# Expert coefficients spread by broadcast loads, the score shift as a bias column, and the order listed anew

## What is computed

```python
x = x + 0.5 * ffn(layernorm(x))
x = x + attn(layernorm(x))        # 16 heads of 8, rotary q and k, ALiBi, full softmax, proj
x = x + 0.5 * ffn(layernorm(x))

def ffn(xf):
    scores = sigmoid(xf @ gate.T)               # 8 experts in 2 groups; the better group is kept
    sel, top = top 2 of (scores + corr_bias) inside the kept group, top normalised to sum 1
    lat = xf @ fc1_w.T                           # 64
    routed = sum over sel of top * (relu(lat @ w1[e].T)**2 @ w2[e].T) @ fc2_w.T
    shared = relu(xf @ up_w.T)**2 @ down_w.T     # 512 wide
    return routed + shared
```

## Time and profile before

| | us |
|---|---|
| median of 3 runs (807.15 to 807.88) | 807.54 |
| profiled execution, its own time | 807.31 |
| span of the profile | 805.5 |
| head, until the first exp starts | 83.85 |
| first to last exp start (256 exps) | 660.8 |
| last exp's start (744.62) to the end of the span | 60.9 |

### The profile page before, as it was taken

One profiled execution on the slowest core, in us unless ns is written; L12 is line 12 of the kernel. 1 busy time (PEld: TensorE's weight loads), 2 busy tenths in 40 slices (PEclk: granted clock), 3 DMA queues, 4 the chain that ended last, 5 costly groups with the idle time before them and its releaser, 6 DMA issues.

```text
span 805.5 us, 14520 instructions
## 1 busy us (share of the span) xinstructions
PE 742.4 (92%) x5520; PEld 370.6 (46%) x5520; DVE 445.9 (55%) x1155; ACT 601.2 (75%) x488; POOL 211.3 (26%) x184
## 2 busy tenths in 40 slices
PE   5996989999999999999999999999989999999876
PEld 3883534444444434344354443443434444434664
DVE  5776445826735773655654656445536435354664
ACT  3892578788878878978878888788878878888321
POOL 2125122223412341332332232321121311211443
PEclk9997799999999999999999999999999999999999
DMA  7015323122166120115332200144322002020200
GB/s 244 1 53 165 104 57 83 28 84 71 42 155 162 46 83 4 33 56 151 77 85 67 55 5 18 47 125 107 71 49 57 5 4 60 4 57 5 60 13 18
DMA packets 43966, 52.60 MB, mean 65 GB/s; under 512 B 10154, under 2 KB 28146, under 8 KB 43762
## 3 DMA queue, kind: packets, MB, share of 16 engines
q1 hardware_dynamic: 42066, 50.19, 23.6%
q10 hardware_dynamic: 1824, 1.41, 0.6%
HBM read 31.91 MB, written 19.40 MB: 64 GB/s over the span
## 4 chain that ended last, share of the span: by engine, by line
PE 67%; ACT 18%; DVE 7%; issue 3%; DMA 1%; POOL 0%; POOLq 0%; DVEq 0%; ACTq 0%
PE f_acc L927 22%; ACT weights L1232 17%; PE f_scores L908 14%; PE f_bank_o L1026 14%; PE f_bank_h L882 9%; PE f_bank_c L1005 1%; DVE weights L1572 1%; PE f_scores L882 1%; PE f_bank_h L951 1%; PE f_bank_c L970 1%; ACT f_relu L1160 1%; PE f_acc L1026 1%; PE f_bank_h L1058 1%; PE f_bank_c L972 1%; DVE f_xn L1327 1%
## 5 line engine op out<-in xcount | busy, mean ns | idle before, releaser
L1232 ACT ACTIVATE weights<-f_scores 128x2048 f32<-128x2048 f32 x256 | 480.8, 1878 | 119.7 <-PE f_scores L908 113.4
L927 PE MATMUL f_acc<-weights,v_res 128*9 128x512 f32 x2048 | 269.9, 596 | 8.8 <-DVE weights L1572 7.2
L1026 PEld LDWEIGHTS f_bank_o<-w_out,f_hid 128*128 128x128 f32 x960 | 121.9, 195 | 59.2 <-issue 50.7
L1026 PE MATMUL f_bank_o<-w_out,f_hid 128*128 128x128 f32 x960 | 146.8, 292 | 1.3 <-POOL f_hid L1270 1.0
L1572 DVE TENSOR_TENSOR weights<-weights,ediag 128x512 f32<-128x512 f32 x128 | 92.7, 724 | 97.8 <-ACT weights L1232 97.3
L1270 POOL TENSOR_TENSOR f_hid<-f_hid,f_relu 128x512 f32<-128x512 f32 x56 | 78.9, 1411 | 201.8 <-DVE f_hid L1462 199.4
L1270 POOL TENSOR_TENSOR f_hid<-f_relu 128x512 f32<-128x512 f32 x56 | 60.5, 1083 | 210.7 <-ACT f_relu L1160 210.6
L908 PE MATMUL f_scores<-q_op,k_plain 29*128 29x512 f32 (+3 forms) x768 | 86.6, 440 | 15.2 <-ACT weights L1232 10.3
L908 PEld LDWEIGHTS f_scores<-q_op,k_plain 29*128 29x128 f32 x768 | 37.4, 183 | 131.6 <-ACT weights L1232 110.6
L1160 ACT ACTIVATE f_relu<-f_bank_h 128x512 f32<-128x512 f32 x110 | 65.4, 595 | 31.2 <-PE f_bank_h L882 30.8
L882 PE MATMUL f_bank_h<-xn_t,w_hi 128*128 128x512 f32 x224 | 83.7, 455 | 5.1 <-ACT f_relu L1160 3.2
(11 more groups left out here) (216 smaller groups left out, 716.1 us busy)
## 6 DMA issues: line engine op xcount, KB each, us to landing
q_parts<-f_parts SPq DMA_DIRECT2D x24, 256.0 KB, 3.0
k_parts<-f_parts SPq DMA_DIRECT2D x24, 256.0 KB, 3.0
q_op<-q_parts SPq DMA_DIRECT2D x48, 96.0 KB
k_full<-k_parts SPq DMA_DIRECT2D x48, 96.0 KB
k_plain<-k_parts SPq DMA_DIRECT2D x48, 96.0 KB
o_scratch<-f_o_out SPq DMA_DIRECT2D x128, 18.0 KB
x_ln<-in_L_attn_x_dram SPq DMA_DIRECT2D x8, 256.0 KB, 3.4
rope<-const_rope SPq DMA_DIRECT2D x1, 2048.0 KB, 10.7
```

Source lines behind the costliest of these rows:

```text
L927: last = nc.tensor.matmul(acc[BLOCK * j:BLOCK * j + VW, :], v_res[:, c // HALVES, kt, col:col + VW], weights[:, n % 2, j, :], start=(kt == ...
L1026: last = nc.tensor.matmul(out_bank(job)[:, t * P:(t + 1) * P], hid[:, m, t * P:(t + 1) * P], w_out[:, m, :], start=(m == 0 and t == 0), st ...
L1232: nc.scalar.activation(weights[:, n % 2, :, :], scores[:, :, :], ACT.Exp).then_inc(exps_done, 1)
```

## The change

1. **13 jobs (A2 to C6) spread the coefficients by DMA.** `turn_coef` transposes 8 rows of `coef` (no high and low part), `take_coef` copies them to `coef_rows` (8x512, VectorE), SyncE stores 16 KB to `coef_scratch` in DRAM two steps after coef, and then loads it back twice, each 64 partitions x 4 tiles x 512 (512 KB), broadcast over the 64 rows of an expert, straight into the expert half of `hid`. The four `spread_coef` products of those jobs are gone (52 in all), `scale` multiplies relu with `hid`, both in SBUF.
2. **The shift is the exp's bias.** `f_shift` and its 32 small DMAs are gone. One product per batch (`cast_bounds`, 128x16) copies the 16 head bounds to all partitions, VectorE reduces them to one column `minus_all` (the minimum, one for all heads of a batch), and each of the 256 exps has that column as its bias.
3. **PLAN is listed anew.** HEAD_STEPS is 216, the last quad's step 471, the last step 504.

```diff
-                nc.scalar.activation(weights[:, n % 2, :, :], scores[:, :, :], ACT.Exp).then_inc(exps_done, 1)
+                batch, first = divmod(n, HALVES * HG * KT)
+                if first == 0:
+                    act.wait_ge(shift_ready, batch + 1)
+                nc.scalar.activation(weights[:, n % 2, :, :], scores[:, :, :], ACT.Exp,
+                                     bias=minus_all[:, batch:batch + 1]).then_inc(exps_done, 1)
...
+            def cast_bounds(job):
+                b = job.batch
+                if not job.head:
+                    bank_h_read("cast", job, 0)
+                else:
+                    pe.wait_ge(norms_read, 2 * HEAD_JOBS)
+                pe.wait_ge(bound_step, 4 * b + 3)
+                nc.tensor.matmul(side_bank(job)[:, 0:HEADS], minus[:, b:b + 1].broadcast_to([HEADS, P]),
+                                 ident[0:HEADS, 0:HEADS], start=True, stop=True).then_inc(bounds_cast, 1)
...
+                    if step == job.at["coef_store"]:
+                        sp.wait_ge(rows_ready, k + 1)
+                        sp.dma_start(env["coef_dram"][job.index], coef_rows[:, :]).then_inc(coef_stored, 16)
+                    if step == job.at["coef_load"]:
+                        sp.wait_ge(coef_stored, 16 * (k + 1))
+                        sp.wait_ge(out_made, HT * job.index)
+                        for side in range(2):
+                            rows = env["coef_dram"][job.index].rearrange("(m s) t -> s m t", s=2)[side:side + 1]
+                            sp.dma_start(hid[INTER * side:INTER * (side + 1), ST:HT, :],
+                                         rows.broadcast_to([INTER, RT, CHUNK])).then_inc(coef_loaded, 16)
...
             def scale(job, m):
+                if job.loads_coef:
+                    dve.wait_ge(coef_loaded, 32 * (job.index - HEAD_JOBS + 1))
+                    v.tensor_tensor(hid[:, ST + m, :], relu_tile(job, ST + m), hid[:, ST + m, :], ALU.mult).then_inc(scaled_ready, 1)
+                    return
...
             def fill_shift(job):
-                v.tensor_scalar(shift[:, :], rope[0:HEADS, 0, 0:CHUNK], 0.0, minus[:, b:b + 1], ALU.mult,
-                                ALU.add).then_inc(shift_ready, 1)
+                dve.wait_ge(bounds_cast, job.batch + 1)
+                v.tensor_reduce(minus_all[:, job.batch:job.batch + 1], side_bank(job)[:, 0:HEADS], AX.X,
+                                ALU.min).then_inc(shift_ready, 1)
```

Two lines of the table, to see what kind of change it is:

```diff
-HEAD_STEPS = 222
+HEAD_STEPS = 216
...
-    ("C", 6, dict(front=(467, 470, 471), norm=(473, 475, 480, 482), route=(483, 484, 485, 486, 487), coef=488,
+    ("C", 6, dict(front=(463, 466, 467), norm=(469, 471, 476, 478), route=(479, 480, 481, 482, 483), coef=484,
```

## The result

The changed kernel takes 838.39 us (median of 4 runs, 833.88 to 840.55) against 807.66: the ratio is 1.0381, interval 1.0354 to 1.0408. That is 31 us slower, where 9 were forecast. The four runs of the changed kernel spread over 7 us, the four of before beside them over 0.7. The execution profiled here has a span of 832.1; it is the fastest of the four, 4.5 us under their median.

A forecast was written before the change was run, and what follows sets the result against it. The loop exp to scores to exp was taken as the bound, a floor of 2.49 us per quad. Terms -5.4 + 1.0 + 19.5 - 4.8 - 2.9 + 1.0 + 2.6 - 1.5 = +9.5 on 807.31 gave 816.8 us, range 804 to 822.

The forecast's parts named there:

- The column: Bias operand on each exp: 78 to 95 ns, taken as 88, in 222 quads at the floor, +19.5 us (17.3 to 21.1).
- Rival (a): The exp's bias column is free, fetched while ScalarE waits 0.6 us for the scores: 797.3 us; chance 0.13.
- The packed steps: Quads that TensorE overfills: 33 in the new table, 9.4 us of excess where it was 14.2, so -4.8 us.
- - 2.9: Three long quads with VectorE's diagonal product late beside GpSimd's squares: -2.9 us if the new order misses them.
- the first two quads: Start of the quads: 2.35 us of excess before, and four hidden groups moved in at half clock, +1.0 (0 to 4).
- Coefficients' way through DRAM: Copy, store and load ahead of the scale: about 8 to 9 us, covered by 10.3 or more, cost nothing.
- Rival (c): Late coefficient load blocks VectorE's scale, then diagonal product, weigh and exp; landing over 10 us behind issue; 822 to 825; chance 0.07.
- New collisions: Scales with both inputs in SBUF, stretched beside GpSimd just ahead of a diagonal product: +1.0 us (0 to 4).
- Casts: Bounds products among the quads wait for the relu behind the exp: about 1.8 at quad 56, 0.8 for batch 2; +2.6 (0 to 4).
- Head: Until the first exp: the shift no longer waits for small DMAs, first exp at 78.4, -5.4 us (-3.5 to -6).
- Tail: Behind the last exp: C6's scales wait for loads, residual +40.7, C7's coefficient turn +46; -1.5 us (-3 to +3).

The follow-up runs named there:

- second profile: The changed kernel run and profiled once more with nothing edited: 838.94 us, ratio 1.0371 to the kernel before.
- before_loads_five: The kernel before with only the coefficient loads, in five jobs (C1 to C5), 20 spread products less: 806.79 us, ratio 0.9999.

## Why the prediction was wrong

**The column: the price of one was right, the sum is so in part by luck.** The 78 to 95 ns from the earlier trace rows are 89. The rule of the Trainium skill ("ScalarE: Activation LUTs", "What ACT_TABLE_LOAD costs") gives about 93 for a pointer operand; the trace agrees to 4 ns. Rival (a) falls: the 0.6 us that ScalarE waits ahead of each exp hide nothing of it. The sum of +19.5 meets 19.6 on the kernel before, and 16.4, 21.4 and 14.3 on three others. But the forecast had 222 quads at the full price, and the pairs of profiles have 153 on the kernel before and some 185 under the new listing, so that the column's own part is 15 to 17 us. What brings the difference up to 20 on the kernel before are falls of TensorE's clock, for which the forecast had no term.

**The packed steps were right.** They have about 7.0 us of excess over 2.58, where the forecast 9.4 less 33 x 0.09 is 6.4.

**The steps that failed are those beside the column.** For the quads the forecast had 19.5 - 4.8 - 2.9 + 1.0 + 1.0 + 2.6 = +16.4; the first profile has +25.9. Of the 9.5 that are missing, taken as excess over the floor, 9.1 are the collisions, 1.4 the casts and 0.6 the packed steps, and the first two quads give 1.6 back (1.7 in place of 2.35 + 1.0). The head lacks 1.3 and the tail 6.2; together that is the 17.1 between +9.5 and +26.6. The second profile has 5 more. One by one:

- *Coefficients' way through DRAM: "It is covered", cost nothing.* In A7 it was not. The steps were read rightly, the load was issued in its step (480.57, in quad 147), and the store had been issued 14 us earlier. What failed is the 10.3 us between the load and the scale four steps on. VectorE keeps to no step where nothing but a semaphore holds it. A7's relus had long been made, so it stood at the scale at 484.86, in quad 149 and not 151, 4.3 us behind the load's issue. The load landed 8.4 behind it. Rival (c) named the mechanism, a scale that blocks and behind it diagonal product, weigh and exp; it set the point at a landing 10 us behind the issue, and 8.4 was enough. In A6 another load paid: the denominators' load, issued behind 1 MB of coefficients, landed after 6.6 us in place of 2.1. The forecast looked at the q/k loads and not at this one.
- *New collisions +1.0 (0 to 4).* They are 10.1: the intervals at quads 12, 65, 101, 102, 153, 154 and 217 over 2.58, with the clock falls that two of them set off. At 12 three scales with both sides in SBUF stand in one step beside three squares. At 101 and 153 late loads pack scales and squares together, and VectorE's operations beside GpSimd are stretched, the routing too (1.50 and 1.37 us for operations that take 0.43 elsewhere). 65 and 217 are the listing's, since they stay with products in place of the loads; 217 is the pattern of the earlier trace rows at a new place. The Trainium skill ("SBUF — State Buffer", "SBUF: two separate sides") says that VectorE with two SBUF inputs and a GpSimd operation that reads SBUF exclude one another. The traces agree for the scales: 0.69 alone and 1.75 to 1.77 where squares run all the while, but 0.69 with one input in PSUM even then. I had the rows for it and set the term by the mild end.
- *Casts +2.6.* The mechanism was right, at 56 and 106. The size is 4.0 (2.9 and 0.3 at quads 56 and 57, 0.7 at 106), and at 56 a fall of the clock is in it.
- *No term for TensorE's clock among the quads.* The earlier trace rows shows 0.99 there and I took it as given. The change thins TensorE's work (52 products less, sparse steps in the listing, 0.09 us more for each exp) and adds waits of 1.6 us and more. Falls that cost 2 to 3 us each follow, some in one profile and not in the next. The listing alone has two and the longer exp alone has two, and none stand in the profile of before or of before_loads_five, which lacks 20 products: so either is enough, and missing products alone have not been seen to do it. The falls make the second profile's 5 us. Whether they make the spread of the first four runs is open. The Trainium skill ("TensorE: Matmul & The Clock Gate", Part 1) says that the gate's observation runs free of the kernel, so that the same work can meet it differently from run to run; the two profiles of one kernel are in line with that.
- *Head -5.4.* It is -4.06 (-3.3 in the second profile). `f_minus` is made at 78.15, not 75.03: A1's second centring starts at 61.24 where it was 58.96, and A2's gate, moved into the head, stands ahead of A1's q and k for 1.7 us at half clock. The rest of the chain, cast 78.44, reduce 79.05, exp 79.79, is as forecast.
- *Tail -1.5.* It is +4.7. "Coef turn as before at +21" was the first error: C5 ends two steps later behind the last quad than before, which was not counted, and C6's turn comes at +23.1. C6's load is issued at +27.7 and lands 7.8 later, so that VectorE waits 2.82 us. The scales take until 40.1 behind the last exp start, where 36 were expected, because the squares run beside them. TensorE waits before and has a clock of 0.50, so that C6's 32 outputs take 6.46 us; C6's residual comes at +45.1 (expected 40.7) and C7's coefficient turn at +51.1 (expected 46). Without any load the tail is 61.7, so 3.4 to 3.9 of it go with the load; C6's and C7's listing as before, with C6's products, gives 1.4 to 2.0.

Reckoned with the medians: before 807.7, the column +19.6, the listing with its casts +8.0 (3 us of head gain inside), the loads +9.0 under this listing: 844. The measured 838.4 is 6 less, and the difference stands between column and listing: on top of the listing the column adds 14.3 and not 19.6. That the falls of the clock that each causes are partly the same ones is likely, and not shown. Five jobs of the kernel before, whose listing gives the loads time, neither lose nor gain by them.

## What to carry to other kernels

On an instruction that stands 256 times on the critical loop, an operand column is priced from any other row of its engine that has one, and it can outweigh all that it makes unnecessary. Work that is hidden beside such a loop is worth nothing when it is removed, and it may be what holds TensorE's clock: look at the busy time of the sparse stretches before thinning them. A place in a list is no time: an engine that nothing holds comes to its step early. So a transfer needs its cover counted from its issue to the moment at which the reader could start. Ask too which small loads stand behind it in the queue, and, where several waits then end at once, what they set off together. And when a forecast term comes out right by the medians, compare the profiles interval by interval before believing it.

## What was not expected of the hardware

The same stretch of work, 8.49 and 8.51 us of TensorE busy in 10.3, was followed in one execution by a granted clock of 0.60 over the next two quads and in another by 1.00. With 147 products more that nobody reads, the kernel's median came out some 5 us lower and not higher, with intervals that leave the size loose. VectorE's 128x512 product with both sides in SBUF takes 0.69 us alone and 1.75 to 1.77 with a GpSimd square beside it throughout, while the same product with one side in PSUM stays at 0.69. And a load of 32 KB that stands in SyncE's queue behind two of 512 KB landed after 6.6 us, where seven others like it have a median of 2.1.
